# Reordering of two stages of an audio-tower kernel: ScalarE's exponentials and GpSimd's half pieces in the first, VectorE's outputs and choice in the last

## The chip, the cores and the metric

One Trainium2 chip, one core. The time is device microseconds of that core, from the start of the program to its end. A run of the profiler gives, beside the time, the span between the first and the last instruction.

## The reference, cut to what matters

`x` has the shape (128, 256, 192), float32. The reference computes three stages for each of the 128 items.

```
# 1 tokenizer: attention pooling over windows of 4 positions, stride 2 (127 windows)
A = tanh(x @ W_w.T + W_b + b);  scores = A @ V_w.T + V_b
w = softmax(scores[:, windows of 4]);  attended = sum over the window of w * x
h = attended @ P_w.T + P_b                       # (128, 127, 192)
# 2 attention with 8 heads on layernorm(h), three mixes of q and k thirds, then a projection
h = h + attn(layernorm(h))
# 3 top-1 mixture of 4 experts on layernorm(h)
z = layernorm(h); e = argmax(softmax(z @ router_w + router_b))
out = h + z + gelu(z @ w1[e] + b1[e], exact) @ w2[e] + b2[e]
```

## The kernel before, in words

The program runs three stages one after the other: `tokenize` (from 0 to about 380 us of the profile), `attend` (to about 1470 us) and `feed_forward` (the rest). Only the first and the last are changed. Every engine has its own instruction queue, executed in program order, and semaphores order the engines against each other. Both stages work on G = 4 items at a time, a group; there are 32 groups.

**First stage.** All engines run a software pipeline whose body i has four slots k = 0 to 3, one item per slot. PE's slot (lines 157 to 186) projects both position parities of item n = 4i + k: five fp16 matmuls of 384 columns for the even half and five for the odd half (L151 to L155). These use high and low fp16 parts of x. It then makes `h` of the item two groups back by multiplying the kept projections `zs` with a banded matrix (`ph<-zs,band`, L184), after waiting for the band from DVE and for an older `h` to have left its PSUM buffer (L182). In slots 1 and 3 a small matmul shifts the scores down or the weights up by one position (`p_shift`, L169 and L174), between the two halves.

ScalarE's slot (lines 203 to 219) issues, in this order: tanh of the projection (L209); a copy of the other half of the projection to `zs`, which waits for PE's L184 of the same slot (L210 and L211); one piece of the fp16 high part of x for the next group (`split`, L199 or L201, 512 columns, four pieces a group); in slot 1 the exponentials of a whole group (`expo<-shifted`, L215), which wait for DVE; and the copy of `h` out of PSUM (L219).

VectorE's slot (lines 303 to 333) makes the two bands (L317) from GpSimd's diagonals, in slots 1 and 2 a part of the softmax (L283 to L288, L292 to L296), then the weighted sums of tanh that give the scores (L326), and the statistics of `h` (L333). L286 writes the negated maximum of the four scores of each window to `least`, and L288 adds it to the scores; L294 writes the reciprocal of the sum to `inv` and L296 multiplies by it. All of `score`, `least`, `expo` and `inv` are in SBUF. `fixed` is a PSUM bank that holds two constants which only VectorE reads.

GpSimd's slot (lines 370 to 395) makes the diagonal (L381) and then one piece of the low part of x for the next group (L389 or L394), piece k in slot k, right after ScalarE has made the high part of the same piece. The SP queue loads the x of group i + 2 when the fourth piece of group i is done (L117).

**Last stage.** Body i of PE (lines 963 on, `up`, `router`, `down`) has six steps c. Step c multiplies group i by a 128-column block of the experts' first weights (`up`, L956 to L960, five matmuls of 512 columns); in step 0 it adds the router of the next group (L938 to L942). Then follows `down` of the block two steps back: steps 0 and 1 finish group i - 1, steps 2 to 5 start group i. `down` of block 0 first waits, for each of the four items, until VectorE has taken the item of the previous group out of its PSUM buffer (`dve_y`, above L970). ScalarE turns each block into `gel` (L1011) and its fp16 high part (L1019), and in steps 0 to 3 first issues one normalization of a later group (L998). VectorE makes the low part of each block (`low`, L1047), chooses the expert from the router's result (`choose`, L1056 to L1073, seven small instructions) and adds the residual to the four finished items (`output`, L1083). GpSimd makes the fp16 halves of x of group i + 2 and packs a part of it (L1117 to L1124, four items a body). The SP queue stores the outputs, transposes the packed choice for group i + 1 (L919) and then x of group i + 2 (L902), in this order.

Of the kernel before, what the change touches and what calls it, by code (L numbers as in the profile page):

```python
# [8 lines left out]
ALU = mybir.AluOpType  # L9
ACT = mybir.ActivationFunctionType  # L10
# [3 lines left out]
CA, CB = 128, 64  # L14
# [12 lines left out]
G = 4  # L27
# [3 lines left out]
def seen(count):  # L31

    return max(count, 0) if isinstance(count, int) else count


def within(x, n):

    return not isinstance(x, int) or 0 <= x < n
# [6 lines left out]
def tokenize(nc, t, dram, NB):  # L45
# [6 lines left out]
    NG = NB // G  # L52
    with ExitStack() as ctx:
# [6 lines left out]
        zs = sb("zs", [128, 2, G, 2, C])  # L60
        tanhs = sb("tanhs", [128, 2, 2 * C])
        score = sb("score", [128, 2, G, 4])
        least = sb("least", [128, G])
        shifted = sb("shifted", [128, G, 4])
        expo = sb("expo", [128, G, 4])
        total = sb("total", [128, G])
        inv = sb("inv", [128, G])
        weight = sb("weight", [128, 2, G, 4])
        weight_up = sb("weight_up", [128, 2, G, 2])
        diag = sb("diag", [128, 2, 2, 128])  # L70
# [11 lines left out]
        p_down, p_up = p_shift[:, 0:2 * G], p_shift[:, 2 * G:4 * G]  # L82
        fixed = ps("fixed", [128, 512])
        vw, below = fixed[:, 0:C], fixed[:, C:C + 128]

        xt_in = [sem("xt_in_even"), sem("xt_in_odd")]
        tok_loaded, loaded, zeroed, built = (sem(n) for n in ("tok_weights_loaded", "weights_loaded", "zeroed", "matrices_built"))
# [12 lines left out]
        def loop(eng, body):  # L100

            for i in range(-1, 3):
                body(i, i % 2, i // 2)
            pairs = (NG - 5) // 2
            with eng.Fori(0, pairs) as j:
                body(j * 2 + 3, 1, j + 1)
                body(j * 2 + 4, 0, j + 2)
            for i in range(3 + 2 * pairs, NG + 3):
                body(i, i % 2, i // 2)
# [79 lines left out]
        @block.scalar  # L189
        def _(act):  # L190
            def split(i, par, half, k):

                if within(i + 1, NG):
                    two = slice(k // 2 * 2, k // 2 * 2 + 2)
                    if k == 0:
                        act.wait_ge(xt_in[1 - par], seen((half + par) * 48 + 48))
                        act.wait_ge(pe_a, seen(i * G))
                    if k % 2 == 0:
                        nc.scalar.activation(xa_hi[:, 1 - par, two, :], xt_a[:, 1 - par, two, :], ACT.Copy).then_inc(act_split, 1)  # L199
                    else:  # L200
                        nc.scalar.activation(xb_hi[:, 1 - par, two, :], xt_b[:, 1 - par, two, :], ACT.Copy).then_inc(act_split, 1)  # L201

            def body(i, par, half):
                for k in range(G):
                    n, two = i * G + k, k % 2
                    if within(n, NB):
                        act.wait_ge(pe_a, seen(n + 1))
                        act.wait_ge(dve_score, seen(n - 1))
                        nc.scalar.activation(tanhs[:, two, :].rearrange("p (o c) -> p o c", o=2), pa[two][:, :, 0:C], ACT.Tanh).then_inc(act_tanh, 1)  # L209
                        act.wait_ge(pe_h, seen(n - 2 * G + 1))  # L210
                        nc.scalar.activation(zs[:, par, k, :, :], pa[two][:, :, C:2 * C], ACT.Copy).then_inc(act_z, 1)  # L211
                    split(i, par, half, k)
                    if k == 1 and within(i - 1, NG):
                        act.wait_ge(dve_shifted, seen(i))
                        nc.scalar.activation(expo[:, :, :], shifted[:, :, :], ACT.Exp).then_inc(act_exp, 1)  # L215
                    u = n - 2 * G - 1
                    if within(u, NB):
                        act.wait_ge(pe_h, seen(u + 1))
                        nc.scalar.activation(t.h[:, bass.ds(u * C, C)], ph[1 - two][:, 0:C], ACT.Copy).then_inc(act_h, 1)  # L219
            loop(act, body)  # L220

        @block.vector
# [115 lines left out]
        @block.gpsimd  # L338
        def _(pool):
            n = 0  # L340

            def diagonal(m, base, value=1.0):

                nonlocal n
                nc.gpsimd.memset(m[:, :], 0.0).then_inc(zeroed, 1)
                n += 1
                pool.wait_ge(zeroed, n)
                nc.gpsimd.affine_select(out=m[:, :], in_=m[:, :], compare_op=ALU.not_equal, fill=value, base=base,
                                        pattern=[[-1, 128]], channel_multiplier=1).then_inc(built, 1)

            diagonal(t.ident, 0)
            diagonal(t.below, -1)
            diagonal(t.above, 1)

            far = t.split["w1"][3][CB:128, :]
            pool.wait_ge(built, 3)
            nc.gpsimd.memset(far, FAR).then_inc(zeroed, 1)
            n += 1
            pool.wait_ge(zeroed, n)
            nc.gpsimd.affine_select(out=far, in_=far, compare_op=ALU.is_ge, fill=0.0, base=0,  # L360
                                    pattern=[[1, NE * HID]], channel_multiplier=-HID).then_inc(zeroed, 1)
            n += 1
            pool.wait_ge(zeroed, n)
            nc.gpsimd.affine_select(out=far, in_=far, compare_op=ALU.is_ge, fill=0.0, base=HID - 1,
                                    pattern=[[-1, NE * HID]], channel_multiplier=HID).then_inc(built, 1)
            pool.wait_ge(built, 4)
            for e in range(NE):
                nc.gpsimd.memset(t.rank[:, :, e:e + 1], float(NE - e))

            def body(i, par, half):  # L370
                for k in range(G):
                    n, two = i * G + k, k % 2
                    u = n - 2 * G + 1
                    if within(u, NB):
                        up, kk = (par, k + 1) if k < G - 1 else (1 - par, 0)
                        if k == G - 1:
                            pool.wait_ge(dve_weight, seen(i))
                        pool.wait_ge(dve_band, seen(u - 1))
                        if k % 2 == 0 and within(i + 1 - (k == 0), NG):
                            pool.wait_ge(pool_split, seen(i * 4 + 4 + k))  # L380
                        nc.gpsimd.tensor_tensor(diag[:, 1 - two, :, :], t.ident[:, :].unsqueeze(1).broadcast_to([128, 2, 128]),  # L381
                                                weight[:, up, kk, 0:2].unsqueeze(2).broadcast_to([128, 2, 128]), ALU.mult)\
                            .then_inc(pool_diag, 1)
                    if within(i + 1, NG):
                        both = slice(k // 2 * 2, k // 2 * 2 + 2)
                        pool.wait_ge(act_split, seen(i * 4 + 5 + k))
                        if k % 2 == 0:
                            pool.wait_ge(pool_split, seen(i * 4 + 4 + k))
                            nc.gpsimd.tensor_tensor(xa_lo[:, 1 - par, both, :], xt_a[:, 1 - par, both, :], xa_hi[:, 1 - par, both, :], ALU.subtract)\  # L389
                                .then_inc(pool_split, 1)  # L390
                        else:
                            if within(u, NB):
                                pool.wait_ge(pool_diag, seen(u + 1))
                            nc.gpsimd.tensor_tensor(xb_lo[0:CB, 1 - par, both, :], xt_b[0:CB, 1 - par, both, :], xb_hi[0:CB, 1 - par, both, :],  # L394
                                                    ALU.subtract).then_inc(pool_split, 1)
            loop(pool, body)


# [432 lines left out]
def feed_forward(nc, t, dram, NB):  # L831
# [4 lines left out]
    with ExitStack() as ctx:  # L836
# [186 lines left out]
        def _(dve):  # L1023
# [20 lines left out]
            def low(i, c):  # L1044
                if within(i, NG):
                    dve.wait_ge(act_hi[c], seen(i + 1))
                    nc.vector.tensor_tensor(glo[:, c % 3, :], gel[:, c % 2, :], ghi[:, c % 3, :], ALU.subtract).then_inc(dve_lo[c], 1)  # L1047
# [28 lines left out]
            def output(i, r, half, k):  # L1076
                if within(i - 1, NG):
                    n = (i - 1) * G + k
                    dve.wait_ge(pe_y, seen(n + 1))
                    dve.wait_ge(pool_x, seen(n + 1))  # L1080
                    if k == 0:
                        dve.wait_ge(stored[(r - 1) % 2], seen(half * 32))
                    nc.vector.tensor_tensor(out_sb[:, (r - 1) % 2, k, :], p_y[k][:, 0:C], res[:, (r - 1) % U, k, :], ALU.add)\  # L1083
                        .then_inc(dve_y, 1)

            def body(i, r, half):
                low(i, 0)
                choose(i, r)
                low(i, 1)
                for k in range(G):  # L1090
                    output(i, r, half, k)
                for c in range(2, HCH):
                    low(i, c)
            loop(dve, body)
# [107 lines left out]
```

## Time and profile before

| | |
|---|---|
| median of 3 runs | 1945.79 us (1943.14 to 1947.16) |
| the profiled execution | 1944.62 us |
| its span | 1942.9 us |
| PE matmul busy | 1802.6 us, 93% of the span |
| DVE busy | 1501.9 us, 77% |
| ACT busy | 1474.9 us, 76% |
| POOL busy | 1258.1 us, 65% |

PE is the busiest engine by far. Its share of busy time in 40 equal slices of the span is 6 at the start, 8 for seven slices, 7 twice, 9 throughout the middle stage, 5 for the slice between the stages and 9 to the end, in tenths. The busy time of a matmul includes the time in which the next one already streams, so two matmuls of 0.33 us can start 0.16 us apart.

### The profile page before, as it was taken

Reading aid. Unit: us, or ns where it says so; the run is one execution under the profiler, and the core shown is the slowest. Engines: PE = TensorE matmul, PEld = TensorE weight load, DVE = VectorE, ACT = ScalarE, POOL = GpSimd, SP = SyncE. Lnnn points to the kernel's source line nnn. Section 1 sums busy time; section 2 is a strip of 40 time slices with the busy share of each in tenths; the row PEclk is TensorE's granted clock in tenths of the full one; section 3 lists DMA queues with packets and bytes.
Section 4 is the critical chain, followed back from the end, with each engine's and each line's share of the span. In section 5 each row is a group of like instructions: output and inputs, shape, how many; then the busy total and the mean of one; then the engine's idle time right before and its main releaser. Section 6 shows DMA issues by size and latency. Waiting matters only on the chain. (4 is left out here: it accounts for less than half of the span.)

```text
span 1942.9 us, 58969 instructions
## 1 busy us (share of the span) xinstructions
PE 1802.6 (93%) x20032; PEld 1007.6 (52%) x20032; DVE 1501.9 (77%) x3674; ACT 1474.9 (76%) x2983; POOL 1258.1 (65%) x2306
## 2 busy tenths in 40 slices
PE   6888888779999999999999999999995999999998
PEld 3556656524444444444444444444443666666666
DVE  6777777768999999999999999999975545454554
ACT  4666666448888888888888888898884666666665
POOL 5666666556777777777777777777744556565651
PEclk9999999969999999999999999999997999999999
DMA  7343343034444444444444444444441322323231
GB/s 185 87 106 89 88 106 86 23 61 82 87 89 89 89 89 89 89 89 88 89 88 89 88 89 88 89 89 89 89 71 35 69 65 63 69 57 75 57 76 47
DMA packets 503935, 159.49 MB, mean 82 GB/s; under 512 B 452176, under 2 KB 503120, under 8 KB 503888
## 3 DMA queue, kind: packets, MB, share of 16 engines
q1 hardware_dynamic: 503888, 158.90, 38.6%
q8 instruction: 26, 0.43, 0.1%
q14 instruction: 21, 0.17, 0.0%
HBM read 37.26 MB, written 12.48 MB: 26 GB/s over the span
## 5 line engine op out<-in xcount | busy, mean ns | idle before, releaser
L740 DVE TENSOR_REDUCE tops<-p_maxa 128x6 f32<-128x762 f32 x512 | 482.2, 942 | 65.6 <-PE p_maxa L578 63.7
L649 PE MATMUL p_o<-probs,vn 127*32 127x256 f32 x6144 | 411.3, 385 | 0.3 <-DVE att L768 0.3
L574 PE MATMUL p_s<-qm,kt 32*128 32x256 f16 x3072 | 399.8, 276 | 2.3 <-DMA qm<-qk 1.3
L692 ACT ACTIVATE probs<-p_s 128x512 f32<-128x512 f32 x512 | 305.4, 596 | 110.5 <-PE p_s L574 96.7
L742 DVE TENSOR_REDUCE tops<-p_maxb 128x4 f32<-128x508 f32 x512 | 345.7, 675 | 0.0
L1047 DVE TENSOR_TENSOR gel_lo<-gel,gel_hi 128x512 f16<-128x512 f32 x192 | 147.2, 767 | 215.5 <-ACT gel_hi L1019 214.1
L698 ACT ACTIVATE probs<-p_s 128x512 f32<-128x512 f32 x512 | 309.0, 604 | 0.0
L695 ACT ACTIVATE probs<-p_s 128x512 f32<-128x512 f32 x512 | 304.6, 595 | 0.3 <-PE p_s L574 0.2
L578 PE MATMUL p_maxa<-kt,qt 24*128 24x256 f16 (+1 forms) x2048 | 283.9, 250 | 17.0 <-DMA qt<-qk 9.0
L793 POOL TENSOR_TENSOR qk<-raw,one 128x384 f16<-128x384 f32 x128 | 105.7, 826 | 222.0 <-ACT raw L716 222.0
L1011 ACT ACTIVATE gel<-f_w,b 128x512 f32<-128x512 f32 x192 | 131.9, 687 | 141.9 <-PE f_w L960 141.8
L574 PEld LDWEIGHTS p_s<-qm,kt 32*128 32x128 f16 x3072 | 135.3, 91 | 184.2 <-issue 165.6
L649 PEld LDWEIGHTS p_o<-probs,vn 127*32 127x32 f32 x6144 | 160.7, 109 | 131.7 <-issue 49.2
L578 PE MATMUL p_maxb<-kt,qt 24*128 24x256 f16 x1024 | 200.5, 275 | 0.1
L1117 POOL TENSOR_TENSOR f_hx<-f_hn,f_one 128x192 f16<-128x192 f32 x120 | 88.3, 736 | 171.3 <-ACT f_hn L998 170.1
L971 PE MATMUL f_y<-w_hi,gel_hi 128*128 128x192 f16 x768 | 188.8, 246 | 0.2 <-DVE gel_lo L1047 0.2
L973 PE MATMUL f_y<-w_hi,gel_lo 128*128 128x192 f16 x768 | 188.9, 246 | 0.0
L972 PE MATMUL f_y<-w_lo,gel_hi 128*128 128x192 f16 x768 | 188.9, 246 | 0.0
L578 PEld LDWEIGHTS p_maxa<-kt,qt 24*128 24x128 f16 x2048 | 109.1, 91 | 139.2 <-PE p_maxa L578 108.0
L184 PE MATMUL ph<-zs,band 128*128 128x192 f32 x512 | 109.6, 337 | 42.5 <-ACT h L219 40.1
L317 DVE SCALAR_TENSOR_TENSOR band<-fixed,weight_up,diag 128x128 f32<-128x128 f32 x256 | 77.4, 344 | 77.5 <-POOL diag L381 76.8
L1019 ACT ACTIVATE gel_hi<-gel 128x512 f16<-128x512 f32 x192 | 120.9, 630 | 7.1
(213 smaller groups left out, 4525.0 us busy)
## 6 DMA issues: line engine op xcount, KB each, us to landing
xt_a<-in_xt SPq DMA_DIRECT2D x32, 512.0 KB, 4.4
xt_b<-in_xt SPq DMA_DIRECT2D x64, 256.0 KB, 5.2
out<-out_sb SPq DMA_DIRECT2D x32, 336.0 KB, 2.7
xt<-hx SPq DMA_TRANSPOSE x128, 2.4
kt<-qk SPq DMA_TRANSPOSE x128, 2.8
qt<-qk SPq DMA_TRANSPOSE x128, 2.4
qm<-qk SPq DMA_TRANSPOSE x128, 2.7
yt<-ay SPq DMA_TRANSPOSE x128, 2.3
```

The costliest lines, as they stand in the source:

```text
L574: return nc.tensor.matmul(o, kt[full(j), r, kind, g, :], qm[full(j), r % 2, versions, g, :], start=True, stop=True, skip_group_check=True)
L578: return nc.tensor.matmul(o, qt[short(j), rq, kind, gm, :], kt[short(j), rk, cols, gm, :], start=True, stop=True, skip_group_check=True)
L649: last = nc.tensor.matmul(p_o[32 * j:32 * j + 32, blocks, :], vn[0:NP, r, src:src + 32], probs[0:NP, r % 2, QUAD * g + j, kind * 256:(kind ...
L692: nc.scalar.activation(probs[:, r % 2, h + 1, 0:512], p_s[1][:, :, :].rearrange("p x n -> p (x n)"), ACT.Exp, scale=SCALE).then_inc(act_e1 ...
L695: nc.scalar.activation(probs[:, r % 2, h:h + 2, 512:768], p_s5[:, :, :].rearrange("p (h x) n -> p h (x n)", h=2), ACT.Exp, scale=SCALE).th ...
L698: nc.scalar.activation(probs[:, r % 2, h, 0:512], p_s[0][:, :, :].rearrange("p x n -> p (x n)"), ACT.Exp, scale=SCALE).then_inc(act_e0[u], 1)
L740: nc.vector.tensor_reduce(top[:, q, pair, 4:10], p_ma[:, 0:6, 0:NP], AX.X, ALU.max, negate=True).then_inc(dve_ma[u], 1)
L742: nc.vector.tensor_reduce(top[:, q, pair, 0:4], p_mb[:, :, 0:NP], AX.X, ALU.max, negate=True).then_inc(dve_mb[u], 1)
L971: nc.tensor.matmul(o, ghi[:, c % 3, n], t.w2_hi[:, c, :], start=False, stop=False)
L972: nc.tensor.matmul(o, ghi[:, c % 3, n], t.w2_lo[:, c, :], start=False, stop=False)
L973: last = nc.tensor.matmul(o, glo[:, c % 3, n], t.w2_hi[:, c, :], start=False, stop=(c == HCH - 1))
L1047: nc.vector.tensor_tensor(glo[:, c % 3, :], gel[:, c % 2, :], ghi[:, c % 3, :], ALU.subtract).then_inc(dve_lo[c], 1)
```

## The change

In the first stage `least` and `inv` become slices of the PSUM bank `fixed`. ScalarE's slot issues `split` ahead of the copy to `zs`, and the exponentials behind the copy of `h`. GpSimd makes the low part of a piece one slot later than before in its own order: slot 0 of body i makes the fourth piece of group i, slots 1 to 3 make the first three of group i + 1. In the last stage VectorE's body goes from `low 0, choose, low 1, outputs` to `low 0, outputs, low 1, choose`.

```diff
-        least = sb("least", [128, G])
-        inv = sb("inv", [128, G])
+        least, inv = fixed[:, 320:320 + G], fixed[:, 320 + G:320 + 2 * G]
@@ ScalarE, first stage
+                    split(i, par, half, k)
+                    if within(n, NB):
                         act.wait_ge(pe_h, seen(n - 2 * G + 1))
                         nc.scalar.activation(zs[:, par, k, :, :], pa[two][:, :, C:2 * C], ACT.Copy).then_inc(act_z, 1)
-                    split(i, par, half, k)
-                    if k == 1 and within(i - 1, NG):
-                        act.wait_ge(dve_shifted, seen(i))
-                        nc.scalar.activation(expo[:, :, :], shifted[:, :, :], ACT.Exp).then_inc(act_exp, 1)
                     u = n - 2 * G - 1
                     if within(u, NB):
                         act.wait_ge(pe_h, seen(u + 1))
                         nc.scalar.activation(t.h[:, bass.ds(u * C, C)], ph[1 - two][:, 0:C], ACT.Copy).then_inc(act_h, 1)
+                    if k == 1 and within(i - 1, NG):
+                        act.wait_ge(dve_shifted, seen(i))
+                        nc.scalar.activation(expo[:, :, :], shifted[:, :, :], ACT.Exp).then_inc(act_exp, 1)
@@ GpSimd, first stage
+            def piece(g, ring, c):
+                if within(g, NG):
+                    two = slice(c // 2 * 2, c // 2 * 2 + 2)
+                    pool.wait_ge(act_split, seen(g * 4 + c + 1))
+                    pool.wait_ge(pool_split, seen(g * 4 + c))
...
@@ in body, around the diagonal L381
-                        if k % 2 == 0 and within(i + 1 - (k == 0), NG):
-                            pool.wait_ge(pool_split, seen(i * 4 + 4 + k))
+                        if k == 1 and within(i, NG):
+                            pool.wait_ge(pool_split, seen(i * 4 + 4))
+                        if k == 3 and within(i + 1, NG):
+                            pool.wait_ge(pool_split, seen(i * 4 + 6))
...
+                    if k % 2 == 0 and within(u, NB):
+                        pool.wait_ge(pool_diag, seen(u + 1))
+                    if k == 0:
+                        piece(i, par, 3)
+                    else:
+                        piece(i + 1, 1 - par, k - 1)
@@ VectorE, last stage
                 low(i, 0)
-                choose(i, r)
-                low(i, 1)
                 for k in range(G):
                     output(i, r, half, k)
+                low(i, 1)
+                choose(i, r)
```

## Rows read from the trace of the kernel before

**Rows 1.** Windows: start:end, length, each engine's busy time (instructions), granted TensorE clock, DMA.
```profile
60.20:360.27 300.07, 263.28 (x1622) 181.69 (x1621) 216.76 (x943) 188.38 (x459) 187.75 (x216) 1.00 0.37 91
360.27:369.78 9.51, 9.51 (x61) 6.71 (x59) 7.51 (x37) 5.53 (x15) 4.73 (x8) 1.00 0.01 2
1507.45:1928.83 421.38, 402.06 (x3760) 288.37 (x3761) 215.67 (x504) 286.73 (x474) 238.78 (x455) 1.00 0.29 65
```

**Rows 2.** Waits of 60.2 to 360.27 us: who waited for whom, total us, times, longest.
```profile
PE ph L184 <- ACT h L219: 36.8, 27, 1.4
```

**Rows 3.** Timeline of PE, one body: start, duration, instruction, idle time before it.
```profile
204.85 0.33 PE L151 MATMUL pa<-wt_ahi,xa_hi 128*128 128x384 f16 x1
...
206.48 0.81 PE L184 MATMUL ph<-zs,band 128*128 128x192 f32 x4
207.13 0.33 PE L151 MATMUL pa<-wt_ahi,xa_hi 128*128 128x384 f16 x1
...
208.08 0.32 PE L151 MATMUL pa<-wt_ahi,xa_hi 128*128 128x384 f16 x1
...
209.67 0.33 PE L151 MATMUL pa<-wt_ahi,xa_hi 128*128 128x384 f16 x1
...
212.83 0.89 PE L184 MATMUL ph<-zs,band 128*128 128x192 f32 x4 [1.37 <-ACT h L219]
213.55 0.33 PE L151 MATMUL pa<-wt_ahi,xa_hi 128*128 128x384 f16 x1
```

**Rows 4.** Timeline of POOL, DVE and ACT in slot 1 of that body.
```profile
211.04 1.15 POOL L394 TENSOR_TENSOR xb_lo<-xt_b,xb_hi 64x512 f16<-64x512 f32 x1 [0.90 <-ACT xb_hi L201]
211.18 1.03 DVE L288 TENSOR_TENSOR shifted<-score,least 128x16 f32<-128x16 f32 x1
...
212.25 0.22 ACT L215 ACTIVATE expo<-shifted 128x16 f32<-128x16 f32 x1 [1.37 <-DVE shifted L288]
212.33 0.61 POOL L381 TENSOR_TENSOR diag<-ident,weight 128x256 f32<-128x256 f32 x1
```

**Rows 5.** Line 288: duration in ns min/median/max, first and last start.
```profile
L288 DVE TENSOR_TENSOR shifted<-score,least x32: 174/1031/1150, 28.7 to 372.8; 128x16 f32<-128x16 f32 x32
```

**Rows 6.** Timeline of ACT in slot 0 of that body.
```profile
206.76 0.49 ACT L209 ACTIVATE tanhs<-pa 128x384 f32<-128x384 f32 x1 [0.47 <-DVE score L326]
...
207.33 0.49 ACT L211 ACTIVATE zs<-pa 128x384 f32<-128x384 f32 x1
...
207.72 0.62 ACT L199 ACTIVATE xa_hi<-xt_a 128x512 f16<-128x512 f32 x1
...
208.23 0.32 ACT L219 ACTIVATE h<-ph 128x192 f32 x1
```

**Rows 7.** Line 120, the loads of x: from issue to landing.
```profile
DMA to landing us min/median/max: 4.1/5.0/9.1
```

**Rows 8.** Waits of 1507.45 to 1929 us.
```profile
PE f_y L970 <- DVE out_sb L1083: 19.8, 31, 0.7
```

**Rows 9.** Timeline of DVE and PE in steps 1 and 2 of a body.
```profile
1714.86 1.02 DVE L1047 TENSOR_TENSOR gel_lo<-gel,gel_hi 128x512 f16<-128x512 f32 x1 [1.38 <-ACT gel_hi L1019]
...
1716.02 0.25 PE L973 MATMUL f_y<-w_hi,gel_lo 128*128 128x192 f16 x1
...
1717.70 0.38 PE L960 MATMUL f_w<-f_pkt,w_blo 128*128 128x512 f16 x1
1718.36 1.14 DVE L1083 TENSOR_TENSOR out_sb<-f_y,f_res 128x192 f32<-128x192 f32 x4
1718.76 0.26 PE L970 MATMUL f_y<-b,f_pkt 128*128 128x192 f16 x1 [0.68 <-DVE out_sb L1083]
```

**Rows 10.** Timeline of SP and PE: x's transposes of that body, the router that reads them.
```profile
1722.48 1.42 SPq L902 DMA_TRANSPOSE f_xt<-f_hx  x1
1727.38 0.17 PE L938 MATMUL f_log<-wrouter_ahi,f_xt 128*128 128x4 f16 x1
```

**Rows 11.** Line 902: from issue to landing.
```profile
DMA to landing us min/median/max: 3.6/3.6/3.8
```

More of the change, by code:

```diff
@@ L368, in _ @@
                 nc.gpsimd.memset(t.rank[:, :, e:e + 1], float(NE - e))
+            def piece(g, ring, c):
[3 more added lines that the diff above has]
+                    pool.wait_ge(pool_split, seen(g * 4 + c))
+                    if c % 2 == 0:
+                        nc.gpsimd.tensor_tensor(xa_lo[:, ring, two, :], xt_a[:, ring, two, :], xa_hi[:, ring, two, :], ALU.subtract)\
+                            .then_inc(pool_split, 1)
+                    else:
+                        nc.gpsimd.tensor_tensor(xb_lo[0:CB, ring, two, :], xt_b[0:CB, ring, two, :], xb_hi[0:CB, ring, two, :],
+                                                ALU.subtract).then_inc(pool_split, 1)
             def body(i, par, half):
@@ L383, in body @@
                             .then_inc(pool_diag, 1)
[L384 to L395, printed above, removed]
+                    if k % 2 == 0 and within(u, NB):
+                        pool.wait_ge(pool_diag, seen(u + 1))
+                    if k == 0:
+                        piece(i, par, 3)
+                    else:
+                        piece(i + 1, 1 - par, k - 1)
             loop(pool, body)
```

## The prediction

> **What bounds the kernel now.** I read the profile's list of busy shares first (table above): PE is at 93%, so time can only go where PE is idle. The slices show that below 9 tenths only in the first stage and between stages. Then the windows over the regular part of each changed stage: 27 bodies of the first take 300.07 us with PE busy for 263.28, and 30 bodies of the last take 421.38 with PE busy for 402.06 [rows 1]. The clock column is 1.00 in all of them, so the clock has nothing to give or take. A body is 300.07 / 27 = 11.11 us in the first stage and 421.38 / 30 = 14.05 us in the last. The waits name one wait of PE in each: for ScalarE's copy of h, 27 times [rows 2], and for VectorE's outputs, 31 times [rows 8]. Both are once a body, and PE has no other recurring wait. These two are what the change can remove.
>
> **First stage: what the stall is.** Write S0 to S3 for the starts of PE's four slots. Slot 0 lasts 207.13 - 204.85 = 2.28 us, slot 1 2.54, slot 2 213.55 - 209.67 = 3.88 [rows 3]. Slot 2 holds the stall: L184 starts 3.16 after its slot instead of 206.48 - 204.85 = 1.63 after. The h it waits for is queued on ScalarE behind the exponentials, which idle for 1.37 until `shifted` is there [rows 4]. And `shifted`, 16 columns, takes 1.03 us: it ends at 212.21, with GpSimd's xb_lo at 212.19 [rows 4]. Over the run the same instruction took from 174 to 1150 ns [rows 5], so its work is about 0.17 us and the rest is waiting for GpSimd's instruction.
>
> **What a body costs without it.** Ten projection matmuls and the four of L184 are slot 0's 2.28 us, back to back. A shift matmul adds, in slot 1, 208.08 - 207.13 - 1.63 / 2 = 0.135, say 0.15, and it comes in slots 1 and 3. So PE needs 4 x 2.28 + 2 x 0.15 = 9.42 us. The last body with projections, 360.27 to 369.78, shows nearly this with the old order: 9.51 us with PE busy for all of it, since there are no pieces of x left for GpSimd to make [rows 1]. I take 9.45.
>
> **Does something else come late at 9.45?** ScalarE, by spacings in slot 0 [rows 6]: tanh at S + 1.91; a copy to zs takes 207.72 - 207.33 = 0.39, tanh I take as the same; a piece takes 208.23 - 207.72 = 0.51; h lasts 0.32. New order: tanh S + 1.91, piece 2.30, zs 2.81 (PE's L184, which it waits for, ends at 1.63 + 0.81 = 2.44), h 3.20 to 3.52. PE's next L184 is due at 2.28 + 1.63 = 3.91, its weights some 0.15 earlier. Slack 0.25 to 0.35 us in every slot. The exponentials now stand behind h and delay only the next tanh, which is due at 2.28 + 1.91 = 4.19, against about 3.7. The exponentials end near S1 + 3.7; DVE's statistics of h and the two bands of slot 2 stand ahead of its three weight instructions; I estimate 0.8 for the former and 0.2 for each of the latter (`shifted` at its shortest, of their size, is 0.17 [rows 5]), so the weights are there near S1 + 5.0; PE's shift wants them at S1 + 2.43 + 2.28 + 0.81 = S1 + 5.52. Slack 0.5.
> GpSimd: per slot one diagonal of 0.61 and one piece of 1.15 [rows 4], 1.76 plus a semaphore of about 0.1, under 2.28 to 2.43. Its piece no longer follows ScalarE's by one instruction, so diagonals come earlier than now and the bands wait less; that gives nothing by itself once PE is the bound. Although a slot later in its queue, the fourth piece ends near S0 + 1.9. PE needs it in slot 2 at S0 + 4.7, and the load of the next but one group starts behind it, near S0 + 2.1. Its three transfers are issued one after the other, I estimate within 1.3 us, and land 5.0 after their issue [rows 7], about S0 + 8.4; ScalarE's piece 0 of that group is at S0 + 9.45 + 2.30 = S0 + 11.75. Hidden by 3.3 us.
> `least` and `inv` in PSUM: the reduction and the reciprocal now write PSUM and two additions read it. This trace has no such write by VectorE. Bounds: nothing, or 0.1 us for each of four instructions; they stand ahead of slack 0.5, so 0 either way, and `shifted` itself drops by 1.03 - 0.17 = 0.86. I take 0 for the sum.
> For `shifted`, the row shows an end tied to GpSimd's. The Trainium skill (SBUF — State Buffer, "Who interferes with whom") states that a VectorE instruction with two SBUF inputs blocks against a GpSimd one that reads SBUF and that one with a single SBUF input does not; by that rule, `shifted` with `least` in PSUM takes its bare duration in every body.
>
> Term: 27 x (11.11 - 9.45) = 44.8 us. From below, PE's recorded idle alone is 300.07 - 263.28 = 36.8; from above 27 x 1.69 = 45.6. Bodies 2 and 3 are loaded with VectorE's preparation of later weights and the drain has a long chain; there I count 2 us (0 to 5). First stage 46.8.
>
> **Last stage.** After `up` of step 2, L970 could start at 1717.70 + 0.215 (five L956 to L960 stream 0.215 apart: 1.08 a step) = 1717.92; it starts at 1718.76 [rows 9], 0.84 late, for a recorded idle of 0.68. So true loss is recorded idle plus 0.165. Over the stage: 19.8 + 31 x 0.165 = 24.9 us [rows 8]. It waits because VectorE works through the seven instructions of the choice and low 1 before the outputs, at 1718.36. In the new order VectorE is free at 1714.86 + 1.02 = 1715.88; PE finishes the first item at 1716.02 + 0.25 = 1716.27 and one more each 0.25 [rows 9]. The outputs take 0.29 each, so they run from 1716.35 to 1717.5: all four are done before 1717.92. Choice and low 1 now fill the time from 1715.88 to 1718.36, 2.48 us together; they follow the outputs to 1720.0. Low 1 comes first and is needed by PE's step 3 only after 1717.92 + 1.33 + 1.08 = 1720.3; low 2, at most 1.02 more, is needed by step 4 at 1720.3 + 0.98 + 1.08 = 1722.4. The choice feeds the SP queue's transpose that stands right ahead of x's (1722.48 [rows 10]) and is for the next body; at 1720.0 it leaves that queue 2.5 us, and the stores of the outputs, first in the queue, come 0.8 us earlier. Cost of the moves: 0 while these slacks hold. Term: 24.9, of which I book 24.5.
>
> The next to come late is x's transpose. It is issued at 1722.48 and lands 3.6 later, at 1726.1 [rows 10, 11]; the router reads it at 1727.38, which becomes 1726.54. Slack 0.45 us. GpSimd's last instruction before it may slip by a few tenths when the choice and low 2 stand beside other instructions of GpSimd than now.
> By the same section of the Trainium skill, whichever of the two starts second blocks fully; by it a low part or a step of the choice could hold GpSimd's chain for its whole length. That makes it a part of rival (c).
>
> **Sum.** 46.8 + 24.5 = 71.3. The profiled execution took 1944.62 for a span of 1942.9, and the median of the runs is 1.2 above it. 1944.62 - 71.3 = 1873.3, and with the 1.2 the median becomes 1874.5; I say 1874. A measurement of this kernel tells differences over 0.2%, 3.9 us.
>
> **Rivals.**
> (a) A new wait in the first stage: h comes later than PE's L184, or the weights later than the shift. For it: h's slack is 0.3 us of a chain of five steps. Against it: the body of 9.51 us. If 0.5 us a body returns, 27 x 0.5 = 13.5: 1888. Chance 12%.
> (b) The PSUM operand doesn't free `shifted`. Then it still ends at about S1 + 3.3, ahead of the exponentials, and eats 0.4 of the 0.5 slack; at the worst 0.3 us a body, 8: 1882. For: no row shows this instruction with a PSUM operand. Chance 6%.
> (c) x's transposes in the last stage bind the router. A slip of 0.75, three quarters of a low part of 1.02 [rows 9] in GpSimd's way, against the slack of 0.45 costs 0.3 x 30 = 9: 1883. Chance 14%.
> (d) One of the two stalls is replaced in full by another wait of its stage: 1898 without the last stage's term, 1921 without the first's. Chance 6%.
> (e) Slower than before. Place: the load of x, since the fourth piece now opens it from slot 0. It costs nothing until it lands 3.3 us later than counted, then each further us costs 27; it cancels all 71 us when it is 3.3 + 2.6 = 5.9 us late, a landing of 10.9 us. The longest shown is 9.1, under the burst of weight loads at the start [rows 7]. Chance 2%, also for the like in the last stage.
> The forecast itself has 60%, with 1868 to 1880 as its own range. The range of 8 in 10 runs from 1868 to 1890, which takes in (a) to (c); (d) and (e) stay outside. Faster by over 0.2%: 96%; within: 2%; slower: 2%.
>
> **What would show it.** In the first stage, no wait of PE L184 for ACT h; `shifted` near 0.2 us; a body of 9.4 to 9.6; POOL's pieces without waits for xa_hi. In the last, no L970 wait for out_sb, a body of 13.2 to 13.3, outputs right after low 0. Wrong if a wait of L184 for h or band, of p_shift for the weights, or of f_log L938 for the DMA stands in each body, or if `shifted` still takes 1 us.

## The result: 1872.3 us, and the profile after

The changed kernel took 1872.34 us (median of 4 runs, 1870.58 to 1873.42) against 1946.23 for the kernel before in the same job: a ratio of 0.9626, 95% interval 0.9611 to 0.9640. The forecast was 1874 with 1868 to 1880 as its own range. The profiled execution has a span of 1871.7 us, 71.2 less than before; the forecast sum was 71.3.

Lines that shifted in the changed kernel: ScalarE's tanh is L208, its piece L198 and L200, zs L212, h L216, the exponentials L219; GpSimd's pieces L377 and L380, its diagonal L396; PE's band product L183, shift of the weights L173. In the last stage the outputs are L1092, `down` L979 to L982, the router's first matmul L947, x's transpose L911.

Windows like those of [rows 1], the first as long as 27 bodies (it begins late in body 3), the second over 30 bodies of the last stage. Columns as there.

```profile
59.50:312.00 252.50, 252.50 (x1617) 186.04 (x1616) 200.99 (x947) 175.80 (x457) 186.43 (x216) 1.00 0.43 108
...
1460.22:1858.70 398.48, 398.25 (x3775) 291.63 (x3774) 223.05 (x511) 287.61 (x475) 234.71 (x456) 1.00 0.31 69
```

PE has next to no idle time left in either: 252.50 of 252.50 and 398.25 of 398.48. Where [rows 2] and [rows 8] had 36.8 and 19.8 us of PE's waits, the waits of 59.5 to 312 us and, below, of the last stage with its start and end (1450 to 1871 us) read:

```profile
ACT tanhs L208 <- PE pa L154: 76.6, 108, 0.9
DVE stats L333 <- ACT h L216: 36.8, 92, 0.9
POOL diag L396 <- DVE weight L296: 31.9, 27, 2.1
POOL xb_lo L380 <- ACT xb_hi L200: 20.6, 46, 0.7
POOL xa_lo L377 <- ACT xa_hi L198: 7.8, 26, 0.3
...
PEld p_shift L173 <- DVE weight L296: 0.3, 1, 0.3
```

```profile
DVE out_sb L1092 <- PE f_y L982: 17.3, 32, 1.3
...
PEld f_log L947 <- DMA f_xt<-f_hx: 2.8, 7, 1.0
PE f_log L947 <- DMA f_xt<-f_hx: 0.8, 2, 0.5
```

The waits turned round: ScalarE waits for PE in 108 slots, GpSimd for the weights once a body, and VectorE's outputs for PE instead of PE for them. GpSimd's pieces still wait for ScalarE's in 72 of the 108 slots, which costs PE nothing: its busy time fills the window. Slot 1 and the start of slot 2 of one body, which answers to [rows 3] and [rows 4]:

```profile
206.18 0.33 PE L150 MATMUL pa<-wt_ahi,xa_hi 128*128 128x384 f16 x1
207.95 0.81 PE L183 MATMUL ph<-zs,band 128*128 128x192 f32 x4
208.01 0.62 POOL L396 TENSOR_TENSOR diag<-ident,weight 128x256 f32<-128x256 f32 x1
208.60 0.33 PE L150 MATMUL pa<-wt_ahi,xa_hi 128*128 128x384 f16 x1
208.85 0.17 DVE L288 TENSOR_TENSOR shifted<-score,fixed 128x16 f32<-128x16 f32 x1
209.23 1.15 POOL L380 TENSOR_TENSOR xb_lo<-xt_b,xb_hi 64x512 f16<-64x512 f32 x1 [0.60 <-ACT xb_hi L200]
209.42 0.33 ACT L216 ACTIVATE h<-ph 128x192 f32 x1
209.63 0.23 ACT L219 ACTIVATE expo<-shifted 128x16 f32<-128x16 f32 x1
```

`shifted` takes 0.17 us and is done at 209.02, 0.2 us before GpSimd's next piece starts. h ends at 209.75; PE's L183 of slot 2 starts at 210.22. In the last stage, what answers to [rows 9]:

```profile
1655.96 1.02 DVE L1056 TENSOR_TENSOR gel_lo<-gel,gel_hi 128x512 f16<-128x512 f32 x1 [1.38 <-ACT gel_hi L1028]
1657.39 1.15 DVE L1092 TENSOR_TENSOR out_sb<-f_y,f_res 128x192 f32<-128x192 f32 x4 [0.42 <-PE f_y L982]
1658.53 0.69 DVE L1056 TENSOR_TENSOR gel_lo<-gel,gel_hi 128x512 f16<-128x512 f32 x1
...
1658.80 0.38 PE L969 MATMUL f_w<-f_pkt,w_blo 128*128 128x512 f16 x1
1659.02 0.25 PE L979 MATMUL f_y<-b,f_pkt 128*128 128x192 f16 x1
```

The outputs end at 1658.54, 0.5 us before `down` wants their buffers, and L979 follows L969 by 0.22 us instead of 1.06.

Where the 71.2 us are, by the start of `first_gap` and `second_gap` (the first VectorE instruction behind the first and the middle stage) in both traces: the first stage ends at 336.1 instead of 380.7, 44.6 us less; the middle one takes 1086.0 instead of 1088.3; the last 449.6 instead of 473.9, 24.3 less. The middle stage has no edit, and in the twelve experiments it takes 1084.7 to 1087.9, so its 2.3 us are of the size by which single executions scatter.

### The profile page after: what moved, and what is told of

Its sections match the earlier page's. It is cut to its first block and busy times, and to the rows that moved or that the text cites. A ratio compares the mean times of both kernels' runs of the same rounds, so it can differ in the third digit from the quotient of the medians.

```text
span 1871.7 us, 59000 instructions
## 1 busy us (share of the span) xinstructions
PE 1789.6 (96%) x20032; PEld 1015.8 (54%) x20032; DVE 1495.4 (80%) x3674; ACT 1462.8 (78%) x2983; POOL 1252.7 (67%) x2306
## 5 line engine op out<-in xcount | busy, mean ns | idle before, releaser
L1056 DVE TENSOR_TENSOR gel_lo<-gel,gel_hi 128x512 f16<-128x512 f32 x192 | 151.0, 787 | 168.9 <-ACT gel_hi L1028 168.7
L982 PE MATMUL f_y<-w_hi,gel_lo 128*128 128x192 f16 x768 | 188.9, 246 | 0.0
L208 ACT ACTIVATE tanhs<-pa 128x384 f32<-128x384 f32 x128 | 62.7, 490 | 99.8 <-PE pa L154 99.8
L396 POOL TENSOR_TENSOR diag<-ident,weight 128x256 f32<-128x256 f32 x128 | 79.2, 620 | 54.2 <-DVE weight L296 45.0
```

Of the source, the lines that this page charges most:

```text
L982: last = nc.tensor.matmul(o, glo[:, c % 3, n], t.w2_hi[:, c, :], start=False, stop=(c == HCH - 1))
```

## The experiments

Theory: each stall is one queue order. In the last stage it is the choice and low 1 ahead of the outputs; in the first the four edits came together, and the runs have to tell which of them removes it. The rival: every edit bears its own part. Each kernel was timed in five rounds against the kernel before, whose median was 1943.4 to 1944.8 us in these jobs; ratios are the safer figures to compare. A body's length is worked out from the starts of the loads of x of bodies 4 to 29, one a body (before 11.13, after 9.36).

**The two stages apart.** `first_only` is the changed kernel with VectorE's old last-stage order; `last_only` the kernel before with the new one.

> The changed kernel with VectorE's old order in the last stage. My theory (the two stages' terms are separate and simply add): the first stage of the changed kernel's trace is 44.6 us shorter than before, so 1946 - 44.6, about 1901 to 1902, ratio 0.977. A rival by which a shorter first stage does something to the later stages (the middle stage read 2.3 us shorter in the two traces): about 1899.

> The kernel before with only VectorE's new order in the last stage. My theory: the wait of the first down matmul for the outputs goes, 24.3 to 24.9 us, so 1921.5, ratio 0.9875, and the router waits for the transpose of x in one body of four, as in the changed kernel, for some tenths. A rival by which this term was partly the first stage's: above 1925.

Measured: `first_only` 1897.37 us, ratio 0.9757 (0.9743 to 0.9771), its last stage 474.1 us long. `last_only` 1920.0, ratio 0.9874 (0.9859 to 0.9889), its last stage 449.6 us, as in the changed kernel. 1 - 0.9757 + 1 - 0.9874 = 0.0369, and both together gave 0.0374: they add. `first_only` came out 4 us lower than expected and so nearer to the rival's 1899. Its trace does not bear the rival out: the middle stage takes 1086.7 us, against 1087.1 in `last_only` with the old first stage. It is the first stage that is shorter, 334.3 us against the 336.1 of the changed kernel, by the start (below).

**One edit of the first stage alone.**

```diff
 exp_only:   the block of L215 (expo<-shifted) moved behind L219 (h<-ph)
 psum_only:  least, inv = fixed[:, 320:320 + G], fixed[:, 320 + G:320 + 2 * G]
 split_only: split(i, par, half, k) moved ahead of L211 (zs<-pa)
 pool_only:  GpSimd's block of the changed kernel (piece(), one slot later)
```

> The kernel before with only the exponentials moved behind the copy of h. Theory A (the three edits of the first stage need each other): h is no longer late, but shifted still ends with GpSimd's piece, so the weights come some 1.4 us after PE's shift matmul wants them, and the wait turns up at p_shift for the weights: gain 0 to 12 us, 1934 to 1946. Theory B (the queue order on ScalarE alone was the stall): gain 35 to 45 us, 1901 to 1911.

> The kernel before with only the minima and the reciprocals in PSUM. Theory A: shifted drops from 1.03 to about 0.2 us, exponentials and h come 0.86 us earlier, gain 27 x 0.86 = 23 us, 1923; L184 still waits for h, some 0.5 us a body. Theory B (the PSUM operand does not free it): shifted stays at 1 us, 1946.

> The kernel before with ScalarE's piece ahead of the copy to zs and nothing else. Theory A: GpSimd's queue stays the chain that bounds (piece, diagonal, band, weights), and gets its piece 0.4 us earlier: at best the 1917 of the changed kernel without GpSimd's new order plus the old last stage, more likely 1925 to 1940. Theory B (ScalarE's order is the cause): 1897.

> The kernel before with GpSimd's pieces a slot later and nothing else. Theory A (GpSimd's order alone is the cause): diagonals no longer stand behind a piece that waits for ScalarE, and with zs ahead of the piece h ends only 0.1 us later than in the changed kernel: 1897 to 1900. Theory B (ScalarE's order is needed as well): a wait of L184 for h stays, 0.3 us or more a body, 1905 or more.

| edit alone | time, ratio (95%) | body | PE's waits in a body |
|---|---|---|---|
| exp_only | 2007.06, 1.0320 (1.0306 to 1.0334) | 11.8 or 13.5, mean 13.3 us | weights, 2.15 us |
| psum_only | 1939.94, 0.9977 (0.9968 to 0.9986) | 10.99 us | h 0.5 and weights 0.5 |
| split_only | 1940.06, 0.9979 (0.9969 to 0.9988) | 10.97 us | h 0.7 and weights 0.4 |
| pool_only | 1902.36, 0.9792 (0.9779 to 0.9806) | 9.51 us | none recorded |

So GpSimd's order alone gives 40 of the 47 us, and each of the other three does little or harm when alone. Theory A on `pool_only` holds but for 2 us: h of slot 1 ends 3.95 us behind the slot's start where it ends 3.57 behind in the changed kernel, and PE's band product of slot 2 starts 0.05 us late and takes 0.89 us instead of 0.81. On `psum_only` I had expected 23 us and got 5: `shifted` did fall to 0.17 us, yet the waits of 100 to 300 us show the same chain a step on, with both ends of it on PE:

```profile
DVE band L316 <- POOL diag L380: 56.6, 73, 1.4
...
PE ph L183 <- ACT h L218: 9.8, 19, 0.5
ACT expo L214 <- DVE shifted L287: 9.4, 18, 0.5
...
PE p_shift L173 <- DVE weight L295: 8.4, 18, 0.5
```

VectorE waits for GpSimd's diagonal in four slots of each body, and the minima, the exponentials and the weights all stand behind those bands in VectorE's queue. By these waits the bound was this loop: ScalarE's piece, GpSimd's piece, GpSimd's diagonal of the next slot, the band, the softmax step behind it, and the wait of ScalarE (and through it its next piece) for that. The stall of [rows 2] was where the loop touched PE.

`exp_only` missed both theories: 62 us slower than before. Its trace, DVE, POOL and PE:

```profile
204.87 1.15 POOL L389 TENSOR_TENSOR xa_lo<-xt_a,xa_hi 128x512 f16<-128x512 f32 x1 [0.92 <-ACT xa_hi L199]
205.00 1.05 DVE L296 TENSOR_TENSOR weight<-expo,inv 128x16 f32<-128x16 f32 x1
...
206.10 0.39 PE L174 MATMUL p_shift<-weight,above 128*128 128x8 f32 x2 [2.15 <-DVE weight L296]
...
206.83 0.49 PE L154 MATMUL pa<-wt_both,xb_hi 128*128 128x384 f16 x1
207.11 0.53 PE L155 MATMUL pa<-wt_low,xb_lo 128*128 128x384 f16 x1
207.43 1.49 PE L184 MATMUL ph<-zs,band 128*128 128x192 f32 x4
```

With h out of the way PE runs ahead until the weights stop it, and now the weights' last instruction also starts just behind a piece of GpSimd's and takes 1.05 us instead of 0.17. PE is idle for 2.15 us, and 0.8 us after it has started again the granted clock falls. Windows of this kernel, the clock in the third column from the end:

```profile
204.00:206.00 2.00, 0.00 (x0) 0.00 (x0) 1.93 (x7) 1.01 (x3) 1.13 (x1) 1.00 0.00 0
206.00:207.00 1.00, 0.90 (x6) 0.64 (x7) 1.00 (x7) 0.00 (x0) 0.63 (x2) 0.93 0.00 0
207.00:208.00 1.00, 1.00 (x4) 0.89 (x3) 0.67 (x3) 0.33 (x1) 0.00 (x0) 0.50 0.00 0
...
209.00:210.00 1.00, 1.00 (x5) 0.46 (x4) 0.00 (x0) 1.00 (x3) 0.00 (x0) 0.50 0.00 0
210.00:211.00 1.00, 1.00 (x7) 0.58 (x6) 0.36 (x1) 0.18 (x1) 0.88 (x1) 0.86 0.00 0
```

0.50 is 1.2 of 2.4 GHz: 3.4 us in which the band product takes 1.49 us instead of 0.81. This happens in 23 of the 26 bodies that have the wait. The other three (waits that end at 74.1, 113.1 and 287.1 us) have the same 2.15 us of idle time and keep 1.00; by the starts of PE's shift matmuls they last 11.8 to 12.0 us and the others 13.5. So the clock takes some 1.7 us a body, about 39 of the 62 us, and the wait for the weights 0.7 us a body against the 11.13 of the kernel before. That kernel idled PE 1.37 us in each body and stayed at 1.00. The Trainium skill (TensorE: Matmul & The Clock Gate, Part 1) tells of an activity monitor that sets the clock by how busy PE has been of late, with 1.2 GHz for an idle one; the level in this trace agrees. Why three bodies kept the clock is not shown.

**The changed kernel with one edit taken back.**

> The changed kernel with the minima and the reciprocals back in SBUF. Theory A: in the changed kernel's trace shifted runs at 208.85 to 209.02, between GpSimd's diagonal (to 208.63) and its next piece (from 209.23), so it meets nothing there: shifted stays near 0.2 us and the time within 1 us of 1872. Theory B, rival (b) of the prediction: shifted takes up to 1 us again and a body loses up to 0.3 us, 1872 to 1880.

> The changed kernel with the exponentials ahead of the copy of h again. Theory A: shifted is done (209.02) before ScalarE reaches that place (209.43), so h comes only the 0.2 us of the exponentials later, inside the slack of some 0.3: within 2 us of 1872. Theory B: any wait ahead of h costs PE in each body, at least 27 x 0.2 = 5 us, 1877 or more.

> The changed kernel with GpSimd's pieces back in their old slot. Theory A: the diagonal of the next slot stands behind a piece that waits for ScalarE, so bands come later, the weights with them, about 0.4 us after the shift matmul wants them: 27 x 0.4 = 11 us, 1883. Theory B: GpSimd's order does not matter once shifted is short, and the start, where VectorE prepares the later weights, is 3 us faster as in the kernel before: 1869.

Measured: `all_but_psum` 1872.98, 0.9638 (0.9625 to 0.9651); `all_but_exp` 1871.75, 0.9628 (0.9615 to 0.9641); `all_but_pool` 1893.07, 0.9741 (0.9728 to 0.9755). Minima back in SBUF and exponentials back ahead of h cost nothing that can be told from the changed kernel's 0.9626. In the first, `shifted` has a median of 174 ns with both inputs in SBUF: at its new place it meets no instruction of GpSimd's in the regular bodies. GpSimd's old order costs 20 us. A body is 10.21 us, and PE waits where the expectation put it:

```profile
202.53 0.17 DVE L296 TENSOR_TENSOR weight<-expo,fixed 128x16 f32<-128x16 f32 x1
...
202.76 0.39 PE L173 MATMUL p_shift<-weight,above 128*128 128x8 f32 x2 [0.57 <-DVE weight L296]
```

The size was low by half: 0.85 us a body, not 0.4. Yet against `last_only` (0.9874) the other three edits together still take off 0.0133, 26 us, without GpSimd's new order, where alone they gave 5, 4 and -62. So the share of an edit depends on its company: GpSimd's order gives 40 us alone and 20 on top of the others.

**Two edits alone.** `pool_split` is the kernel before with `piece()` and `split` moved, nothing else.

> The kernel before with two edits of the first stage: GpSimd's pieces a slot later and ScalarE's piece ahead of the copy to zs. Exponentials ahead of h, minima in SBUF, last stage as before. Theory A (these two are the whole effect, since taking away either of the others from the changed kernel cost nothing): a body of 9.37 us, 1897, ratio 0.976. Theory B (each of the other two edits can stand in for the other, so without both the stall returns): shifted meets GpSimd again in some bodies and h waits for the exponentials, 1905 to 1930.

Measured: 1897.38 us, 0.9756 (0.9743 to 0.9769), body 9.37 us: the whole of `first_only` (0.9757). Theory A holds. Of its 0.0244, GpSimd's order alone gives 0.0208; ScalarE's `split` adds 0.0036, 7 us, once GpSimd's order is new, and 0.0021 when alone. The medians put that at 5.0 us, and the shorter body (9.51 to 9.37 by the loads) gives 27 x 0.14 = 3.8 us; what is left is inside the intervals of the two ratios.

**The last stage: what stood in the way.**

```diff
 choose_first, VectorE's body, last stage, in the changed kernel
                 low(i, 0)
+                choose(i, r)
                 for k in range(G):
                     output(i, r, half, k)
                 low(i, 1)
-                choose(i, r)
```

> The changed kernel with VectorE's last-stage order low 0, choice, outputs, low 1. It tells whether the choice or low 1 held the outputs up. Theory A: the choice is 1.95 us of the 2.48 us and ends at 1717.75 in the old trace, so outputs end 0.6 us earlier than with the old order, of a lateness of 0.84: some 0.25 us a body stay, 8 us, 1880. Theory B (low 1 alone was the cause): 1872.

Measured: 1882.52 us, 0.9685 (0.9672 to 0.9698); last stage 459.9 us against 449.6. Theory A, and near its 8 us: the choice accounts for 10 of the 24 us when low 1 is out of the way, low 1, by subtraction, for the other 14. The order with low 1 alone ahead of the outputs was not run.

**The start.** I took VectorE for its bound, which prepares the later weights in bodies 0 to 2 beside GpSimd's pieces. Instructions of both kernels in 20 to 60 us, before first (columns as in the page's list: busy and mean ns):

```profile
L260 DVE CAST w_bhi<-w_b 128x768 f16<-128x768 f32 x1 | 0.5, 548 | 0.0
L270 DVE CAST bproj<-bprojf 1x192 f16<-1x192 f32 x1 | 0.3, 251 | 0.0
```

```profile
L260 DVE CAST w_bhi<-w_b 128x768 f16<-128x768 f32 x1 | 1.5, 1507 | 0.0
...
L270 DVE CAST bproj<-bprojf 1x192 f16<-1x192 f32 x1 | 1.2, 1202 | 0.0
```

The load of body 4 is issued at 65.62 us in the changed kernel, 62.82 before; yet kernels with the very same first stage have it at 63.84 (`first_only`) and 62.23 (`choose_first`). Two things differ in these starts. VectorE's 27 instructions for the later weights take 16.3 us in all in the kernel before and 20.7 in the changed one (21.2 in `first_only`, 19.0 in `choose_first`). And the granted clock is at 0.50 for 3.4 us before, at 26 to 30 us, but for 10.2 in the changed kernel and in `first_only`, and for 6.8 in `choose_first`. In the changed kernel the second fall comes behind a wait of PE for the weights:

```profile
47.92 0.39 PE L173 MATMUL p_shift<-weight,above 128*128 128x8 f32 x2 [2.44 <-DVE weight L296]
48.98 1.17 PE L183 MATMUL ph<-zs,band 128*128 128x192 f32 x4
...
51.53 0.53 PE L150 MATMUL pa<-wt_ahi,xa_hi 128*128 128x384 f16 x1
```

From 49.3 to 52.6 us PE then streams without a pause at half rate. Neither figure alone puts the starts in order: `all_but_exp`, with 18.2 us of VectorE's instructions and 6.8 us at 0.50, issues this load at 64.67. How the 3 us are shared between the two is not shown. `act_casts` tests the first of them and moves the 16 casts to ScalarE:

```diff
+            def casts(s):
...
+                    nc.scalar.activation(w[0][:, :], a[:, :], ACT.Copy)
+                    nc.scalar.activation(t.third[name][:, :], c[:, :], ACT.Copy)
+                    nc.scalar.activation(w[2][:, :], b[:, :], ACT.Copy).then_inc(high, 1)
...
+                    if isinstance(i, int) and 3 <= n < 12 and n % 2 == 1:
+                        casts(n - 3)
...
-                        nc.vector.tensor_copy(w[0][:, :], a[:, :])
-                        nc.vector.tensor_copy(t.third[name][:, :], c[:, :])
-                        nc.vector.tensor_copy(w[2][:, :], b[:, :]).then_inc(high, 1)
```

> The changed kernel with the 16 casts of the later weights (the high parts) on ScalarE, one slot later, in place of VectorE; the low parts stay on VectorE. Theory A (the start, up to body 4, is bound by VectorE, whose casts meet GpSimd's pieces: they took up to 1.57 us where their shortest are 0.25 to 0.74): the start gets 3 to 8 us shorter, 1864 to 1869. Theory B (ScalarE's casts delay h and tanh as much): within 2 us of 1872.

Measured: 1870.29 us, 0.9621 (0.9608 to 0.9634), the load of body 4 at 61.97, the granted clock at 0.50 for 6.8 us before it. By the times it is not to be told from the changed kernel (0.9626, 0.9611 to 0.9640), so the gain of 3 to 8 us did not come; a gain of 1 or 2 us stays open. VectorE then waits for ScalarE's casts instead: its waits of 20 to 60 us have `DVE w_alo L278 <- ACT w_bhi L211` with 1.9 us. It has the lowest median of all, by less than the measurement tells. So the stretched casts are not shown to be what sets the start.

## Why the prediction was right

By its own steps:

- *The stalls and what a body costs without them.* Right. The forecast had 9.45 and 13.2 to 13.3 us; measured 9.36 and 397.39 / 30 = 13.25 (L979 of bodies 1 and 31 start at 1460.22 and 1857.61). The 9.42 worked out from the slots was 0.06 high, and rounding it up to the 9.51 of the last body cost a little more: 27 x 0.09 = 2.4 us of under-forecast.
- *Nothing else late.* Right, with the slacks nearly as worked out, with S1 = 206.18: h ends at S1 + 3.57 (forecast 3.52), the weights at S1 + 5.12 (forecast 5.0), the load of x starts at S0 + 2.1 (206.01 with S0 = 203.91), as said. One sign failed: GpSimd's pieces were to run without waits for ScalarE's, and they wait in 72 of 108 slots, for 28.4 us in all. PE lost nothing by it.
- *The start and the drain.* Wrong: booked as a gain of 2 us. In the profiled execution body 4 starts 3.4 us later than before (63.52 against 60.12, by its load less 2.1 and 2.7 us), and the drain gave back 0.8, so with 27 x (11.11 - 9.36) = 47.2 the first stage gave 44.6, not 46.8. The failed step is that the 2 us had no row of their own: I looked at the clock only in the windows of [rows 1], where it is 1.00, and put no term for VectorE's instructions there taking longer. In the start of the changed kernel VectorE's instructions for the later weights take 4.4 us more and the clock stays at 0.50 for 6.8 us more; the cause of either and the share of each stay open. From profile to profile this term is between about +1 and -3.
- *PSUM.* The price was right (0.17 to 0.19 us for the four instructions). The benefit was ascribed wrongly: the stall was told as `shifted` behind GpSimd's piece, and that is true of the trace before, but freeing it alone gave 5 us, and leaving it in SBUF in the changed kernel lost nothing. The wrong sentence was that "diagonals come earlier than now and the bands wait less; that gives nothing by itself once PE is the bound": it is the larger part of what makes PE the bound. The order of GpSimd's queue alone gave 0.0208 of the 0.0243 of `first_only`, 40 of 47 us. The total did not suffer, since all four edits were there and the sum was made against PE's own need: it was right whichever edit removed the stall.
- *The last stage.* Right: 24.3 us against 24.5. Rival (c) showed itself in one body of four, after the loop's branch, with 2.8 us of waits of PE's weight loads and 0.8 of PE in all.
- *Rival (b)*, that the PSUM operand does not free `shifted`, is refuted by `psum_only`, where all 32 take 0.170 to 0.172 us with GpSimd's old order; and `all_but_psum` shows that its price of 8 us does not arise in the changed kernel (0.9638 against 0.9626). Rivals (a), (d) and (e) did not occur.

The first and the last stage together gave 68.9 us, 2.4 less than the 71.3 forecast; the span fell by 71.2 only because the unchanged middle stage happened to be 2.3 us shorter in this execution. That the two agree to 0.1 us is luck. What stays open is the size of the start's term in the medians, since the profiles of kernels with the same first stage differ by 3.4 us there, and why.

## What to carry to other kernels

The wait that stands ahead of PE names where a loop touches PE, not which link of it is long: before crediting an edit, follow the loop through every in-order queue, and ask whether an instruction that waits for a fresh input stands ahead of one that others wait for. Putting the late-fed piece one slot back in GpSimd's queue was worth 40 us alone and 20 beside the other edits, while moving only the exponentials, which stood ahead of the h that the wait named, made the kernel 3% slower, for the greater part by the clock. Edits of one loop do not add: each has to be tried alone and taken back alone. The size of a gain is best taken from what the bounding engine needs per body, checked against a body of the same trace that happens to run without the disturbance.

## What was not expected of the hardware

In `exp_only` PE idles 2.15 us in each body, and in 23 of 26 bodies the granted clock falls from 1.00 to 0.50 for 3.4 us behind it; 1.37 us in each body of the kernel before did not do it once. The regular windows at 1.00 said nothing about the start, where the changed kernel spends 10.2 us at 0.50. A VectorE instruction of 16 columns took 1.05 us when it began 0.13 us behind a GpSimd instruction of 1.15 us, and casts with a single SBUF input stretched too: one of 768 columns took 0.55 us when it began 0.2 us ahead of GpSimd's piece, which then took 1.35 us instead of 1.15, and 1.51 us when it began 0.2 us behind one. The Trainium skill (SBUF — State Buffer, "Who interferes with whom") names casts among those that can take the port pair shared with GpSimd, in a mode that uses both ports; these durations agree with it.
